# A macaron block: attention scores once, by query, with the probabilities transposed by DMA

## What is computed

```python
x = x + 0.5 * ffn(layernorm(x))
x = x + attention(layernorm(x))      # 32 heads of 16, window 128
x = x + 0.5 * ffn(layernorm(x))

# attention, for a block of 128 queries and the 256 keys of its block and the one before:
scores = (q @ k.T) / sqrt(16); scores = where(0 <= query - key <= 128, scores, min)
out = softmax(scores) @ v @ Wo.T
# ffn, 512 -> 2 x 2048 -> 512, ternary weights (per group of 64) and an RMS norm of the hidden row:
h = silu(x @ Wgate.T) * (x @ Wup.T);  y = rms_norm(h) @ Wproj.T
```

## Time and profile before

| | |
|---|---|
| median of 3 runs | 2278.78 us (2277.72 to 2279.49) |
| the profiled execution | 2278.95 us, of it 2277.2 us span |
| PE busy | 2063.2 us, 91% of the span |
| DVE busy | 1784.5 us, 78% |
| ACT busy | 1401.9 us, 62% |
| POOL busy | 768.5 us, 34% |
| DMA queue q1 | 25.7% of 16 engines |
| mean granted TensorE clock | 0.961 |

### The profile page before, as it was taken

The page is one execution under the profiler, slowest core; times in us unless marked ns, Lnnn a source line. Parts: engine busy times, 40 slices in busy tenths (PEclk is TensorE's granted clock), DMA queues, the critical chain, the costliest instruction groups (busy, mean ns, idle before and its releaser), DMA issues. The chain is left out here.

```text
span 2277.2 us, 64890 instructions
## 1 busy us (share of the span) xinstructions
PE 2063.2 (91%) x26752; PEld 1496.5 (66%) x26752; DVE 1784.5 (78%) x4393; ACT 1401.9 (62%) x2073; POOL 768.5 (34%) x963
## 2 busy tenths in 40 slices
PE   1327789999999999999999999999999999999877
PEld 1315557777777777777777767777777777776556
DVE  8965678787887788877887878878878888887764
ACT  5523357665676566765767566765666566666672
POOL 4431123332333333333333333333333233333332
PEclk9668889999999999999999999999999999999989
DMA  4221222222332222222322222332223222223210
GB/s 161 74 83 29 52 47 53 53 48 57 57 50 44 46 48 57 57 53 48 57 58 54 39 46 49 57 57 52 48 57 57 57 36 46 49 52 48 43 34 20
DMA packets 351269, 121.62 MB, mean 53 GB/s; under 512 B 336128, under 2 KB 336128, under 8 KB 350464
## 3 DMA queue, kind: packets, MB, share of 16 engines
q1 hardware_dynamic: 350976, 117.47, 25.7%
HBM read 25.17 MB, written 8.39 MB: 15 GB/s over the span
## 5 line engine op out<-in xcount | busy, mean ns | idle before, releaser
L778 DVE CUSTOM_DVE_ANT_0 masked<-ps_s,mask 128x256 f32<-128x256 f32 (+1 forms) x1024 | 338.4, 386 | 199.3 <-PE ps_s L983 199.1
L622 ACT ACTIVATE prob<-ps_s,neg_exp_scale 128x512 f32<-128x512 f32 (+1 forms) x512 | 295.9, 629 | 123.2 <-PE ps_s L997 123.2
L504 POOL TENSOR_TENSOR acc_A<-acc_A,sq 128x512 f32<-128x512 f32 x96 | 125.7, 1310 | 568.2 <-ACT sq L639 568.0
L536 ACT ACTIVATE hid<-ps_g 128x512 f32<-128x512 f32 x256 | 151.8, 593 | 259.9 <-PE ps_g L950 259.8
L752 DVE TENSOR_TENSOR pt<-prob,pt 128x1024 f16<-128x1024 f32 (+1 forms) x256 | 276.8, 1081 | 6.9 <-ACT pt L614 6.9
L1007 PE MATMUL ps_y<-wp_t,h_hi 128*128 128x512 bf16 x1024 | 267.2, 384 | 14.9 <-ACT h_hi L532 14.9
L504 POOL TENSOR_TENSOR acc_C<-acc_C,sq 128x512 f32<-128x512 f32 x96 | 134.0, 1395 | 434.8 <-ACT sq L639 434.8
L645 ACT ACTIVATE prob<-prob,prob_bias 128x1024 f32<-128x1024 f32 (+1 forms) x256 | 265.0, 1035 | 0.6
L1007 PE MATMUL ps_y<-wp_t,h_lo 128*128 128x512 bf16 x1024 | 264.6, 381 | 0.0
L950 PE MATMUL ps_g<-xt_C,wgu_t 128*128 128x128 f16 x4096 | 255.0, 221 | 7.4 <-DMA xt_C<-xh 6.8
L950 PE MATMUL ps_g<-xt_A,wgu_t 128*128 128x128 f16 x4096 | 260.5, 224 | 1.3 <-DMA xt_A<-xh 1.3
(11 more groups left out here) (152 smaller groups left out, 3311.3 us busy)
## 6 DMA issues: line engine op xcount, KB each, us to landing
stream<-in_L_attn_x_dram SPq DMA_DIRECT2D x32, 256.0 KB, 3.7
out_dram<-stream SPq DMA_DIRECT2D x32, 256.0 KB, 2.5
stream<-in_L_ffn_w_gate_up_dram SPq DMA_DIRECT2D x4, 1024.0 KB, 5.2
prob<-in_L_ffn_w_gate_up_dram SPq DMA_DIRECT2D x4, 1024.0 KB, 5.6
stream<-in_L_ffn_w_proj_dram SPq DMA_DIRECT2D x2, 1024.0 KB, 4.9
prob<-in_L_ffn_w_proj_dram SPq DMA_DIRECT2D x2, 1024.0 KB, 4.8
stream<-in_L_attn_Wq_dram SPq DMA_DIRECT2D x1, 1024.0 KB, 5.4
prob<-in_L_attn_Wk_dram SPq DMA_DIRECT2D x1, 1024.0 KB, 7.6
```

Of the source, the lines that this page charges most:

```text
L504: pool.tensor_tensor(out=acc[s][:, :], in0=acc[s][:, :], in1=sq[:, step % 2, :], op=ALU.add).then_inc(g_acc[s], 1)
L536: act.activation(hid[:, step % 2, :], ps_g[:, :], ACT.Tanh, scale=0.5 * 2.0 ** -XS_LOG2).then_inc(a_tanh[s], 1)
L622: act.activation(halves(prob[:, g % 2, 4 * o:4 * o + 4, :], b), halves(score_bank(step, 2 + o).rearrange("p (t q) -> p t q", q=P), b), ACT ...
L778: m = dve.tensor_tensor_reduce(masked[:, g % 2, 2 * pair + o, first:2 * P], score_bank(step, o)[:, pair * 2 * P + first:(pair + 1) * 2 * P ...
```

## The change

The second product is gone, and the attention is computed from the first. `masked_max` still adds the mask and takes the maxima, and the masked scores that it writes are now used: in the same step ScalarE makes a bias of a group's four maxima (`exp_bias`, 128 x 4) and takes the exponential of each head in place, with a `[128,1]` scale and a `[128,1]` bias. One step later it copies the high part to `prob`, GpSimd subtracts it for the low part, and a DMA on SyncE's queue transposes both parts to `pt`; two steps after the scores TensorE multiplies with v. The windows' `affine_select`, the second transposition of q, `max_rows`, the Relu and VectorE's low part of the probabilities are dropped. A block leaves after 34 steps, and there are 282. The accumulator of squares has a PSUM bank of its own. In the weights' stage GpSimd drops out: ScalarE spreads each group's scale over a row (`spread`), and VectorE does `differ`'s subtraction and all twelve sign products.

```diff
-    SCORES_T = 20
-    PROB = SCORES_T + 1
-    PV = SCORES_T + 2
+    PROB = SCORES + 1
+    PV = SCORES + 2
...
-    SPLIT_O, WO_AT = NORM + 7, 31
-    LN_C, XHAT_C, SPLIT_C = 32, 33, 34
-    UP_C, SQ_C, ADD_C = 36, 40, 41
+    SPLIT_O, WO_AT = NORM + 7, 23
+    LN_C, XHAT_C, SPLIT_C = 24, 25, 26
+    UP_C, SQ_C, ADD_C = 28, 32, 33
...
         @block.sync
...
-                b = block_at(step, M_AT)
-                if b is not None:
-                    sp.wait_ge(d_m, b + 1)
-                    sp.wait_ge(p_s, 16 * b + 16)
-                    transpose(qt[:, b % QRING, :, :], q4[:, b % 2, :, :, :].rearrange("p a b c -> p (a b c)"), t_qm)
+                b, g = group_at(step, PROB)
+                if b is not None:
+                    sp.wait_ge(g_pl, 8 * b + g + 1)
+                    need(sp, p_pv, 8 * b + g - 1)
+                    first = first_half(b)
+                    transpose(pt[:, g % 2, first:2, :, :, :].rearrange("p a b c d -> p (a b c) d"),
+                              prob[:, g % 2, first:2, :, :, :].rearrange("p a b c d -> p (a b c d)"), t_p[g % 2])
...
         @block.gpsimd
...
-            for n in range(NTU):
-                differ(n)
-                if n % 2 == 0 and n > 0:
-                    give_sign(n - 1)
...
+                b, g = group_at(step, PROB)
+                if b is not None:
+                    pool.wait_ge(a_ph, 8 * b + g + 1)
+                    pool.tensor_tensor(out=prob_part(prob[:, g % 2, :, 1, :, :], b), in0=prob_f32(b, g),
+                                       in1=prob_part(prob[:, g % 2, :, 0, :, :], b),
+                                       op=ALU.subtract).then_inc(g_pl, 1)
...
         @block.scalar
...
+            def spread(n):
+                act.wait_ge(w_grp, n + 1)
+                need(act, w_dif, n)
+                act.activation(w_wide.rearrange("p (g k) -> p g k", g=G64),
+                               grp_scale[:, n % 2, :].unsqueeze(2).to_broadcast([P, G64, 64]),
+                               ACT.Copy).then_inc(w_spread, 1)
...
+                b, g = group_at(step, PROB)
+                if b is not None:
+                    act.wait_ge(a_exp, 8 * b + g + 1)
+                    need(act, t_p[g % 2], 16 * (4 * b + g // 2))
+                    act.activation(prob_part(prob[:, g % 2, :, 0, :, :], b), prob_f32(b, g), ACT.Copy).then_inc(a_ph, 1)
+
                 for s, offset in SPLITS:
...
+                b, g = group_at(step, SCORES)
+                if b is not None:
+                    act.wait_ge(d_mx, 16 * b + 2 * g + 2)
+                    need(act, a_exp, 8 * (b - 1) + g + 1)
+                    act.activation(exp_bias[:, 4 * g:4 * g + 4], row_max[:, 4 * g:4 * g + 4], ACT.Identity,
+                                   bias=prob_bias[:, 0:1], scale=neg_exp_scale[:, 0:1]).then_inc(a_bias, 1)
+                    act.wait_ge(a_bias, 8 * b + g + 1)
+                    for h in range(4):
+                        p = masked[:, g % 2, h, P * first_half(b):2 * P]
+                        t = act.activation(p, p, ACT.Exp, bias=exp_bias[:, 4 * g + h:4 * g + h + 1],
+                                           scale=exp_scale[:, 0:1])
+                    t.then_inc(a_exp, 1)
+
                 s, b, c = ffn_at(step)
                 if s and not (s == "A" and b == 0):
                     tanh_half(s, b, c, step)
...
         @block.vector
...
+                dve.wait_ge(w_spread, n + 1)
+                need(dve, w_q[n % 2], n // 2)
+                dve.tensor_tensor(out=diff, in0=w_wide, in1=w, op=ALU.subtract).then_inc(w_dif, 1)
...
-                b, g = group_at(step, PROB)
-                if b is not None:
-                    take_lo(halves(pt[:, 1, g % 2, :, :], b), halves(prob[:, g % 2, :, :], b),
-                            halves(pt[:, 0, g % 2, :, :], b), a_ph, 8 * b + g + 1, d_pl)
...
         @block.tensor
...
-                b, g = group_at(step, SCORES_T)
-                if b is not None:
-                    need(pe, a_neg, 2 * groups_by(step - 1, SCORES_T))
-                    need(pe, d_mx, 2 * groups_by(step, SCORES) - (group_at(step, SCORES)[0] is not None))
-                    if g == 0:
-                        pe.wait_ge(t_qm, 16 * (b + 1))
-                    scores_t(b, g, step)
...
-                    pe.wait_ge(d_pl, 8 * b + g + 1)
+                    pe.wait_ge(t_p[g % 2], 16 * (4 * b + g // 2 + 1))
```

200 lines of the change are left out of this document (70 added, 130 removed).

## The result

The changed kernel takes **2449.55 us** (median of 4 runs, 2448.35 to 2450.68) against 2278.25 (2277.25 to 2279.49) for the kernel before: a ratio of **1.0752, 95% interval 1.0733 to 1.077**. It is slower, as forecast, but by 171 us instead of 57, and outside the range of 2245 to 2410.

What follows compares the result with a forecast made beforehand. A 7.50 us ring of VectorE and ScalarE replaces TensorE as the bound, 66.45 us a block: +58.6 for blocks, -28.6 weights' stage, +15 filling and draining, +12 clock, +57 on 2279, so 2336 us; range 2245 to 2410.

Steps and rivals of the forecast that it cites:

- The ring: Each step's chain through VectorE and ScalarE: maxima, bias, exponentials, Tanh, gated, hidden, h_hi, h_lo, next maxima; 7.50 us.
- Rival 1: ScalarE's exponentials: two pointer operands cost as one, step 0.45 us shorter, 2246 us; chance 0.14 including what lies towards the forecast.
- The stage of the weights: Weights' stage before the blocks: GpSimd no longer works beside VectorE, 28.6 us saved.
- So at nothing: GpSimd's subtraction of 1024 columns: at most 2.8 us, beside other work, with about 2 us of slack before `prob_v`.
- Step 6: Step of each block where `oh` stands ahead of the bias in ScalarE's queue: 2.0 us more, some 11 us long.
- The first blocks of a sequence: Half-width first block of each sequence: 0.97 us a step less, 60.6 us a block.
- filling and draining: Pipeline's start and end, where no FFN runs: 6 us added at the start and 9 at the end.
- the 12 us set aside: Lower TensorE clock after step 6's wait: 1.7 us in each of 7 first blocks.
- rival 3: TensorE's clock falls in every block, some 3.5 us more each, +98 us, 2434 us; chance 0.08.
- The transposed probabilities: DMA transposition on SyncE's queue ahead of `prob_v`: 4.4 us for 16 tiles, some 60% of the engines, not late.
- rival 4: Transposing DMA lands in 8.8 us, `prob_v` waits 2.4 us a step, about +500 us; chance 0.03.
- Two signs of being right: In the profile after: TensorE idles about 9 us a block before `ps_g`; VectorE's busy share falls by some 300 us.

Runs made afterwards that it cites:

- the run without the low part: Changed kernel with GpSimd subtracting one column instead of 128x1024 and the low parts of the probabilities zeros written once: 2373.75 us, ratio 1.0417.
- Tanh-first: Changed kernel with ScalarE's Tanh ahead of the bias and four exponentials of the same step: 2233.74 us alone; other versions add further edits.
- VectorE's low part in the first queue order: Changed kernel, Tanh first, VectorE taking the probabilities' low part, SyncE issuing their transposition ahead of those of xh and oh: 2277.93 us.

## Why the prediction was right and wrong

- **The ring, 7.50 us: right**, link by link (7.51 in the rows above). So is its cause: the Tanh behind the exponentials. That both pointer operands count was the choice on which the sign hung, made between 0.28 and 0.37 us of fixed cost; measured are 0.589 us for an exponential against 0.585, and 93 ns less with one operand fewer. Rival 1 falls with it; its price, by its own terms, was 3.0 us a block and not 3.2 (3.6 in three full blocks, 1.3 down to TensorE's 59.3 in a first one). The Trainium skill ("ScalarE: Activation LUTs", "What ACT_TABLE_LOAD costs") says that each `[128,1]` pointer operand adds about 93 ns; the trace agrees.
- **The stage of the weights, 28.6 us: right** (27.5 alone). VectorE's comparison L674 took 3.480 us beside GpSimd and takes 1.225 without, as assumed.
- **"So at nothing", said of GpSimd's subtraction: this step failed**, by 75.8 us of the 113. I priced its length (at most 2.8 us; it takes 2.15) and its chain to `prob_v`, which does have slack (`prob_v` waits 19.2 us for the transposed probabilities in the whole run, and 19.4 without the subtraction). What I did not ask is what stands *behind* it in GpSimd's queue and who works *beside* it. Behind it stand the powers of `add_ffn`: 37.2 us. Beside it VectorE's xh and o_norm take 1.41 for 0.72 us and 0.82 for 0.30: 38.6 us. The forecast's own rows had the warning: L674 beside GpSimd 3.480, L683 undisturbed 1.225. I used it as a gain in the stage of the weights and not as a cost in the blocks. On the contention the Trainium skill ("GPSIMD Engine Reference", "1. Specifications") says that GpSimd shares its SBUF interfaces with VectorE, in contention with VectorE instructions in a 2-port perf mode or with two SBUF inputs. The trace agrees for xh and o_norm, which have two. It also shows an operation with one tensor input slowed by other work of GpSimd: xhat of B and C, 29 of 32 times beside the adding of squares, takes 1.41 to 1.42 us in the mean, with the subtraction or without it, and xhat of A 0.54; in which mode it runs no row tells.
- **Step 6: right in form, 0.9 us short.** Its oh starts 3.71 us after the maxima began where the forecast took 2.99 from the earlier trace rows; the difference is the low part of xh, which is ahead of it and now 1.40 us. Without the subtraction xh takes 0.69 again, and the step is 10.98 against the forecast's 10.80.
- **The first blocks of a sequence, 60.6 us: this term was sized too small, by 3.3 us each.** The forecast shortened every step by 0.97 us. In the run without the low part their eight steps sum to 63.9 us, and steps 0 and 1 are 8.52 and 8.41 instead of 7.6 and 7.8. In the two Tanh-first runs with the powers first or the subtraction gone they are 8.64 and 8.41 or 8.42, though the ring is open. So these steps are not the ring's, but TensorE's, which has an `up`, a `down` and a projection in them: the ring's length had been taken where another bound was nearer. 3.3 us in each of 7 such blocks are 23 us; full blocks without the subtraction are 0.9 us too long, 19 us in 21; filling and draining without it are 3 and 5 us above the forecast. Less the 12 us set aside and the 1.5 us gained at the start, these 50 make the 37 us that the subtraction leaves of the 113.
- **The clock: rival 3 half true.** From 700 to 1900 us the granted clock is 0.96, above the 0.93 that the forecast had named as its sign; the kernel before has 1.00, and so have the Tanh-first versions, except the one with VectorE's low part in the first queue order (0.98). It falls to the lower of its two levels (1.2 instead of 2.4 GHz) where TensorE has waited: after 2.44 us of waiting, an `up` in a step 6 takes 2.52 and 3.06 us, at a granted clock of 0.75 and 0.62, where its fellows in the next step take 1.96 and 1.95 at 1.00.

```profile
1168.61 2.52 PE L927 MATMUL ps_g<-xt_C,wgu_t 128*128 128x128 f16 x32 [2.44 <-DVE hid L755]
1170.93 3.06 PE L927 MATMUL ps_u<-xt_C,wgu_t 128*128 128x128 f16 x32
```

  The Trainium skill ("TensorE: Matmul & The Clock Gate", "Why this matters for your kernels") warns against idle gaps between bursts of matmuls, after which the clock is back at half; the trace agrees in kind. But with the same 0.96 the run without the low part has full-width steps within 0.2 us of the forecast, so I take most of the slow matmuls to run in time that TensorE would have spent waiting; no run holds the clock up to test it. How much of the 0.9 us a full block, and of the 8 us of filling and draining, is the clock's, stays open.
- **The transposed probabilities: not late**, as forecast. They land in 4.3 us, and the queue takes 47.8% of the engines, where the forecast had some 60%. Something like rival 4 does appear once the low part is late: then the issue waits at the head of SyncE's queue.
- **Two signs of being right came out otherwise.** TensorE idles 129.5 of the 1200 us from 700 on, 7.6 us a block against about 9 forecast, but not mainly before `ps_g` (88.8 us in the whole run): 111.8 us are before `down`, for `add_ffn`, the wait that the forecast did not have. And VectorE's busy time fell by 151 us instead of 300, since xh and o_norm took 132 us more. The first scores (197.0 against some 199), the exponential (0.589) and step 6 as the longest are as forecast.

## What to carry to other kernels

When an engine's queue gets a wait and a long piece of work in one place, list what stands behind it: here the Tanh behind the exponentials (216 us), a 0.55 us power behind a subtraction (37 us, or 79 us once the ring was open), and a transposition behind another's wait (84 us). The amount of work was the same each time. An engine with free time is not a free place: price work on GpSimd by what VectorE runs beside it, too. And where a chain sets some steps and an engine's own work others, take the larger of the two step by step, and only then the mean.

## What the runs showed of the hardware

- A subtraction on GpSimd, 128x1024, float32 and float16 in, float16 out, takes 2.15 us in the mean. VectorE's operations with two inputs in SBUF that run beside it take up to 2.21 us instead of 0.69 (low part of xh, 128x512), and up to 2.20 instead of 0.29 (multiply of o_norm, 128x128). The multiply below, which began 0.12 us after a subtraction of 2.13 us, lasted as long as all of it, so the delay is not in proportion to VectorE's own size:

```profile
1020.45 2.15 DVE L787 TENSOR_TENSOR o_norm<-o_sum,row_inv 128x128 f32<-128x128 f32 x1
```

  That row is from the run with only the Tanh moved.
- VectorE does the same subtraction in 1.22 us. Its maxima, which have one input in PSUM, take 0.42 us beside GpSimd's subtraction and away from it. An operation with one tensor input, the xhat of 128x512, takes 0.54 us alone and 1.50 beside GpSimd's adding of squares.
